# Spectral bank without turns in its slots, and V loads of 96 and 4 rows in neighbourhood attention

## The chip, the cores and the metric

The kernel runs on one core of a Trainium2 chip. The metric is the device time of one execution in microseconds. TensorE is called PE, VectorE DVE, ScalarE ACT, GpSimd POOL and SyncE SP, as in the profile.

## The reference

The input x is (2, 128, 64, 64) in fp32. Four layers in a row each add something to it: neighbourhood attention over 7 x 7 windows (twice, then a layer norm), a convolution attention, linear attention and a spectral filter bank, causal attention and experts. Two of them are changed. Neighbourhood attention, per image, layer and head:

```python
attn = jnp.einsum('bijhd,bijpqhd->bijhpq', q, kw)      # kw, vw: the 7 x 7 windows
attn = softmax(attn + bias over the 49 keys)
out = jnp.einsum('bijhpq,bijpqhd->bijhd', attn, vw) @ w_p.T + b_p
```

The spectral bank takes u (2, 4096, 128), the layer norm of the tokens, and 16 filters phi of 4096 positions:

```python
U_plus = irfft(Vf[None, :, :, None] * Uf_p[:, :, None, :], n=8192)[:, :sl]   # and U_minus with signs
out = einsum('btkd,k,kde->bte', U_plus, s, Mpp) + einsum('btkd,k,kde->bte', U_minus, s, Mpm)
out = out + sum over i < 3 of (u shifted by i) @ Mu[i]                        # three taps
```

This is done for prefixes of four lengths, weighed by a gumbel softmax and summed.

## The kernel before

X, the 128 channels by 2 x 4096 positions, stays on chip for the whole kernel. The stages follow each other with barriers between them. Order is written out by hand: each stage has one program for each engine, and semaphores link them.

**Neighbourhood attention** (`neighbourhood_attention`) has four passes (two layers, two images) of 32 groups each, 128 in all. ACT stores V to DRAM tile by tile (`v_out`, two buffers). SP copies it there into overlapping windows (`group`: 12 DMAs for a quarter of a pass, lines 270 to 273), and loads the windows of each group (`load`, line 282, `na_v`, four buffers, 100 rows of 1040 values). PE multiplies in `values` (line 365). The loads, the window copies and their waits all stand in SP's one queue. Ahead of it all, the input is group normed. PE's part of that is one matmul (line 415), behind the bias tables (lines 401 and 405) in PE's program.

**The spectral bank** replaces the long FFT by blocks: the 4096 positions are 64 blocks of 64 (`NB`, `R`). A transform over the block index gives 64 slots, each slot a pair of rows. In every slot the convolution within blocks is a product with filter rows laid out as a Toeplitz matrix.

- `spectral_inputs` stores u to DRAM (line 1379) and loads it with blocks as rows (line 1384). PE transforms the filters (line 1413) and u (line 1421), DVE drains, SP stores `u_hat`.
- `autoregressive` adds the three taps (line 1723), one loop body per image.
- `spectral_slots` runs the 64 slots, each of 4 chunks (`kc`). PE turns the slot's input (`turn_inputs`, line 1528), multiplies it with the filters (`convolve`, line 1542, into five PSUM banks) and mixes over filters and channels with the mixing weights (`mix`, lines 86 to 88). Values are split in a high and a low fp32r part, and each product is three matmuls. ACT makes the high part of a convolution's result (line 1589), DVE the low part (line 1624), POOL splits the filters. PE convolves a chunk of the next slot while it mixes this slot's, four chunks ahead, and turns the output (`turn_outputs`, line 1562) before SP stores it.
- `spectral_inverse` loads `y_hat` (line 1666), transforms back over blocks and stores it. `spectral_output` loads that with positions as rows, turns it on PE and adds it to X times `keep`, a factor for each 512 positions.

## Time and profile before

| | us |
|---|---|
| median of 3 runs (3557.59 to 3560.82) | 3558.94 |
| the profiled execution | 3560.56 |
| its span in the profile | 3558.8 |
| PE busy | 3162.1 (89%) |
| DVE busy | 1884.2 (53%) |
| ACT busy | 1281.8 (36%) |
| POOL busy | 989.8 (28%) |

Busy is the time in which an engine had an instruction at work. The shares are means over stages that differ: in the profile's slices PE has a 9 (90% or more) all through the slots, and lower digits around them.

### The profile page before, as it was taken

Reading aid. Unit: us, or ns where it says so; the run is one execution under the profiler, and the core shown is the slowest. Engines: PE = TensorE matmul, PEld = TensorE weight load, DVE = VectorE, ACT = ScalarE, POOL = GpSimd, SP = SyncE. Lnnn points to the kernel's source line nnn. Section 1 sums busy time; section 2 is a strip of 40 time slices with the busy share of each in tenths; the row PEclk is TensorE's granted clock in tenths of the full one; section 3 lists DMA queues with packets and bytes.
Section 4 is the critical chain, followed back from the end, with each engine's and each line's share of the span. In section 5 each row is a group of like instructions: output and inputs, shape, how many; then the busy total and the mean of one; then the engine's idle time right before and its main releaser. Section 6 shows DMA issues by size and latency. Waiting matters only on the chain. (4 is left out here: it accounts for less than half of the span.)

```text
span 3558.8 us, 60876 instructions
## 1 busy us (share of the span) xinstructions
PE 3162.1 (89%) x23681; PEld 2437.8 (69%) x23681; DVE 1884.2 (53%) x3818; ACT 1281.8 (36%) x2479; POOL 989.8 (28%) x976
## 2 busy tenths in 40 slices
PE   5998988688864789999999999999788998999799
PEld 4676776233433258888888888888457886888655
DVE  5555565577525345555555555555235554555365
ACT  2554544111222034444444444444233333333300
POOL 3444441277421034444444444444000000000000
PEclk9999999799986899999999999999889999999899
DMA  6877751000012643444434444443410000000000
GB/s 164 178 156 168 157 149 48 12 1 1 1 34 82 219 68 62 73 71 64 75 63 72 71 64 75 65 70 62 154 46 1 1 1 1 1 1 1 8 18 30
DMA packets 431206, 230.12 MB, mean 65 GB/s; under 512 B 328468, under 2 KB 409004, under 8 KB 427724
## 3 DMA queue, kind: packets, MB, share of 16 engines
q1 hardware_dynamic: 408352, 212.60, 29.2%
q10 hardware_dynamic: 22572, 13.63, 1.8%
q8 instruction: 192, 3.15, 0.4%
q14 instruction: 90, 0.74, 0.1%
HBM read 186.20 MB, written 61.28 MB: 70 GB/s over the span
## 5 line engine op out<-in xcount | busy, mean ns | idle before, releaser
L1624 DVE TENSOR_TENSOR sl_vl_slot<-sl_psV_slot,sl_vh_slot 128x512 fp32r<-128x512 f32 x1024 | 635.7, 683 | 553.7 <-ACT sl_vh_slot L1589 553.7
L1589 ACT ACTIVATE sl_vh_slot<-sl_psV_slot 128x512 fp32r<-128x512 f32 x1024 | 529.5, 604 | 536.5 <-PE sl_psV_slot L1542 536.2
L86 PE MATMUL sl_psY_slot<-sl_vl_slot,sp_Mh_sp 128*128 128x256 f32 x2048 | 603.3, 295 | 0.0
L87 PE MATMUL sl_psY_slot<-sl_vh_slot,sp_Ml_sp 128*128 128x256 f32 x2048 | 578.4, 282 | 0.0
L88 PE MATMUL sl_psY_slot<-sl_vh_slot,sp_Mh_sp 128*128 128x256 f32 x2048 | 577.4, 282 | 0.0
L86 PEld LDWEIGHTS sl_psY_slot<-sl_vl_slot,sp_Mh_sp 128*128 128x128 f32 x2048 | 390.0, 190 | 56.3 <-issue 56.3
L1516 POOL CAST sl_fh_slot<-sl_f_slot 128x512 fp32r<-128x512 f32 x256 | 168.7, 659 | 864.2 <-PE sl_psV_slot L1542 686.8
L87 PEld LDWEIGHTS sl_psY_slot<-sl_vh_slot,sp_Ml_sp 128*128 128x128 f32 x2048 | 390.9, 191 | 0.0
L88 PEld LDWEIGHTS sl_psY_slot<-sl_vh_slot,sp_Mh_sp 128*128 128x128 f32 x2048 | 390.3, 191 | 0.0
L1518 POOL TENSOR_TENSOR sl_fl_slot<-sl_f_slot,sl_fh_slot 128x512 fp32r<-128x512 f32 x256 | 338.1, 1321 | 20.5
L1914 PE MATMUL ca_ps_ca<-ca_v_ca,ca_pt_ca 128*128 128x128 f32 x2112 | 285.6, 281 | 25.1 <-ACT ca_pt_ca L2003 14.2
L1914 PEld LDWEIGHTS ca_ps_ca<-ca_v_ca,ca_pt_ca 128*128 128x128 f32 x2112 | 258.2, 194 | 42.2 <-ACT ca_pt_ca L2003 25.8
L1542 PE MATMUL sl_psV_slot<-sl_fl_slot,sl_uh_slot 64*128 64x512 f32 x1024 | 230.6, 447 | 2.1 <-POOL sl_fl_slot L1518 1.1
L2003 ACT ACTIVATE ca_pt_ca<-ca_ps_ca 128x512 f32<-128x512 f32 (+2 forms) x144 | 82.6, 573 | 370.0 <-PE ca_ps_ca L1904 370.0
L1542 PE MATMUL sl_psV_slot<-sl_fh_slot,sl_ul_slot 64*128 64x512 f32 x1024 | 203.7, 394 | 0.0
L1542 PE MATMUL sl_psV_slot<-sl_fh_slot,sl_uh_slot 64*128 64x512 f32 x1024 | 200.4, 388 | 0.0
L691 POOL TENSOR_TENSOR na_s_na<-na_s_na,na_nmax_na 128x400 f32<-128x400 f32 x128 | 109.1, 853 | 278.0 <-DVE na_nmax_na L575 257.7
L1981 DVE COPY ca_pt_ca<-ca_ps_ca 128x512 f32<-128x512 f32 (+1 forms) x144 | 91.0, 632 | 179.5 <-PE ca_ps_ca L1904 178.9
L365 PE MATMUL na_psO_na<-na_v_na,na_pt_na 100*64 100x129 f32 x2048 | 144.9, 285 | 34.7 <-issue 34.7
L1904 PE MATMUL ca_ps_ca<-ident,ca_s_ca 128*128 128x128 f32 x1056 | 156.3, 276 | 4.3 <-ACT ca_s_ca L1993 4.3
L365 PEld LDWEIGHTS na_psO_na<-na_v_na,na_pt_na 100*64 100x64 f32 x2048 | 113.5, 140 | 61.0 <-issue 54.3
L1952 DVE TENSOR_SCALAR_CACHE_REDUCE ca_s_ca<-ca_ps_ca 128x512 f32<-128x512 f32 x224 | 149.0, 688 | 0.8 <-PE ca_ps_ca L88 0.8
(383 smaller groups left out, 5608.1 us busy)
## 6 DMA issues: line engine op xcount, KB each, us to landing
sl_f_slot<-filt_hat SPq DMA_DIRECT2D x256, 256.0 KB, 5.5
na_v_na<-na_windows SPq DMA_DIRECT2D x128, 406.2 KB
na_windows<-na_values SPq DMA_DIRECT2D x160, 113.8 KB, 7.2
na_values<-na_vo_na ACTq DMA_DIRECT2D x32, 260.0 KB, 8.9
u_hat<-fw_o_fwd SPq DMA_DIRECT2D x8, 1024.0 KB, 3.8
sl_u_slot<-u_hat SPq DMA_DIRECT2D x128, 64.0 KB, 2.1
y_hat<-sl_o_slot SPq DMA_DIRECT2D x64, 128.0 KB, 1.8
iv_y_inv<-y_hat SPq DMA_DIRECT2D x8, 1024.0 KB, 12.0
```

Of the source, the lines that this page charges most:

```text
L86: e.matmul(out, lh, rl, start=start, stop=False)
L87: e.matmul(out, ll, rh, start=False, stop=False)
L88: return e.matmul(out, lh, rh, start=False, stop=stop)
L365: mm = e.matmul(psO[side:side + 64, u // 2, u % 2 * 129:(u % 2 + 1) * 129], pt_sb[g % 2][0:NK, u, side:side + 64], v_in[g % NV][0:NK, s, 0 ...
L1516: e.tensor_copy(high, raw).then_inc(S["f_high"], 1)
L1518: e.tensor_tensor(low, raw, high, ALU.subtract).then_inc(S["f_split"], 1)
L1542: mm = e.matmul(psV[(first + par) % NPV][:, :], u_in[u % 2][pu][rows, b, :], f_in[kc][pf][rows, :], start=(x == 0), stop=(x == 2))
L1589: e.activation(v_out(0, kc, q), bank(n), ACT.Copy).then_inc(S["v_high"], 1)
L1624: e.tensor_tensor(v_out(1, kc, q), bank(n), v_out(0, kc, q), ALU.subtract).then_inc(S["v_split"], 1)
L1904: tr = e.transpose(psT[n % 2][:, j * 128:(j + 1) * 128], s_sb[i % 2][:, at:at + 128], T["ident"][:, :])
L1914: mm = e.matmul(psO[i % 2][:, 0:128], pt_sb[n % 3][:, j, :], v_all[:, k, :], start=(k == 0), stop=(k == i))
L1952: e.tensor_scalar(dst, psS[n % 3][:, 0:k], 1.0, None, ALU.mult, ALU.max, accum_out=m)\
```

## The change

In neighbourhood attention each burst of 12 window copies is cut in three parts, and SP issues a V load between them. A V load becomes two DMAs, of 96 rows and of 4. There are five `na_v` buffers for four, four `v_out` buffers for two, and the group norm's matmul stands ahead of the tables.

In the spectral bank `spectral_inputs` no longer goes through DRAM for the blocks. PE turns them: columns of u at a stride of 64 values (256 bytes) are the weights, the identity moves, and the result, after a copy by ACT, is the transform's moving operand. The filters' transform and the taps follow in the same stage. `u_hat` is stored with positions as rows, so a slot needs no turn of its input; POOL splits it. PE runs two chunks ahead instead of four, with six PSUM banks and three buffers each for filters and results. The output is stored as it is, in runs of 256 bytes, and image 0's part is loaded again every eight slots (`load_early`). The last two stages become `spectral_outputs`: y at a stride of 256 bytes is the weights, the inverse matrix times `keep` moves with 64 columns, and DVE adds the result straight into X.

```diff
@@ -185,7 +184,7 @@
     PASSES = [(layer, b) for layer in range(2) for b in range(B)]
     G = PER * len(PASSES)
     STEPS = 3 * NCH
-    NQ, NS, NP, NV = 3, 3, 2, 4
+    NQ, NS, NP, NV, NO = 3, 3, 2, 5, 4
...
-                def group(n, part):
-                    for i in range(2):
-                        e.wait_ge(S["v_stored"][i], 16 * ((n * NCH + 2 * part) // 2 + 1))
+                def group(n, part, third):
+                    if third == 0:
+                        for i in (n * NCH + 2 * part, n * NCH + 2 * part + 1):
+                            e.wait_ge(S["v_stored"][i % NO], 16 * (i // NO + 1))
...
-                    for k in range(WIN):
+                    for k in range(4 * third, min(4 * third + 4, WIN)):
...
+                    if third == 2:
+                        e.dma_start(windows[:, :, 0, :], V[:, 0:WIN, :]).then_inc(S["v_grouped"][part], 16)
+                        e.dma_start(windows[:, :, SUB - 1, :], V[:, W - WIN:W, :]).then_inc(S["v_grouped"][part], 16)
...
+                    keys = T["v_windows"][n, k0:k0 + WIN, :, half * 2 * UNITS:(half + 1) * 2 * UNITS, :].rearrange("r k s d -> (r k) s d")
+                    for rows in (slice(0, 96), slice(96, NK)):
+                        e.dma_start(v_in[g % NV][rows, :, :], keys[rows]).then_inc(S["v_loaded"][g % NV], 16)
...
-                    if g in (NV + 1, NV + 5):
-                        group(0, 2 + g // (NV + 5))
+                    if NV <= g < NV + 6:
+                        group(0, 2 + (g - NV) // 3, (g - NV) % 3)
                     for n in range(1, len(PASSES)):
                         for part in range(PARTS):
-                            if step_slot(n * STEPS + 6 * part + 5) + 4 == g:
-                                group(n, part)
+                            third = g - step_slot(n * STEPS + 6 * part + 5) - 4
+                            if 0 <= third < 3:
+                                group(n, part, third)
+
...
-                    e.wait_ge(S["v_loaded"][g % NV], 16 * (g // NV + 1))
+                    e.wait_ge(S["v_loaded"][g % NV], 32 * (g // NV + 1))
...
+                e.wait_ge(S["mom_done"], 1)
+                e.matmul(psO[:, 1, 0:2 * B], T["gmat"][:, :], mom[:, :, :].rearrange("p b m -> p (b m)"),
+                         start=True, stop=True).then_inc(S["grp_in_psum"], 1)
                 e.wait_ge(S["mask_loaded"], 16 * 9)
                 e.wait_ge(S["pick_done"], 1)
                 tables(0)
-                e.wait_ge(S["mom_done"], 1)
-                e.matmul(psO[:, 1, 0:2 * B], T["gmat"][:, :], mom[:, :, :].rearrange("p b m -> p (b m)"),
-                         start=True, stop=True).then_inc(S["grp_in_psum"], 1)
...
+                def turn(c):
+                    if c >= 2:
+                        e.wait_ge(S["t_copied"], c - 1)
+                    for i in range(SC):
+                        s = c * SC + i
+                        for b in range(B):
+                            blocks = G["U"][:, b, UPAD + s:UPAD + s + (NB - 1) * R + 1:R]
+                            mm = e.matmul(psT[c % 2][b * NB:(b + 1) * NB, (SC - 1 - i) * 128:(SC - i) * 128], blocks,
+                                          T["ident"][:, :], start=True, stop=True)
+                    mm.then_inc(S["t_in_psum"], 1)
+
+                def ring_free(n):
+                    if n >= 4:
+                        e.wait_ge(S["f_dve"] if n % 2 else S["f_act"], (n - 4) // 2 + 1)
+
+                def transform(c):
+                    e.wait_ge(S["t_copied"], c + 1)
+                    for b in range(B):
+                        ring_free(2 * c + b)
+                    for b in range(B):
+                        rows = slice(b * NB, (b + 1) * NB)
+                        e.matmul(ps[(2 * c + b) % 4][:, :], fwd[rows, b, :], turned[c % 2][rows, :], start=True, stop=True)\
+                            .then_inc(S["f_in_psum"], 1)
+
+                e.wait_ge(S["fwd_loaded"], 16)
+                for c in range(NS):
+                    turn(c)
+                    if c >= 1:
+                        transform(c - 1)
+                transform(NS - 1)
                 e.wait_ge(S["phi_loaded"], 32)
+                for n in range(NU, NU + NFT):
+                    part, k0 = divmod(n - NU, 4)
+                    ring_free(n)
+                    e.matmul(ps[n % 4][:, :], flt[:, part, :], phi[:, 4 * k0:4 * k0 + 4, :].rearrange("a k m -> a (k m)"),
+                             start=True, stop=True).then_inc(S["f_in_psum"], 1)
+                for n in range(B * NCH):
+                    b, c = divmod(n, NCH)
+                    if n >= 2:
+                        e.wait_ge(S["ar_added"], n - 1)
+                    for i in range(3):
+                        at = UPAD + c * CH - i
+                        mm = e.matmul(psA[n % 2][:, :], G["Mu"][:, i, :], G["U"][:, b, at:at + CH], start=(i == 0), stop=(i == 2))
+                    mm.then_inc(S["ar_in_psum"], 1)
...
-    NPV = 5
+    CHUNKS = SLOTS * KC
+    NPV, NFI, NVR, EARLY = 6, 3, 3, 8
...
-                    for b in range(B):
-                        e.dma_start(u_raw[u % 2][:, b, :].rearrange("d (i s) -> d i s", i=2), uh[u, :, b, :, :].rearrange("i d s -> d i s"))\
+                    uh = T["u_hat"][2 * u:2 * u + 2, :, :].rearrange("i (s q) c -> q i s c", q=2)
+                    for par in range(2):
+                        e.dma_start(u_raw[u % 2][par * R:(par + 1) * R, :, :].rearrange("p b d -> p (b d)"), uh[par])\
...
+                    for b in range(B):
+                        e.dma_start(T["y_hat"][2 * u:2 * u + 2, b, :, :].rearrange("o e r -> e o r"),
+                                    y_sb[u % 2][:, b * 128:(b + 1) * 128].rearrange("e (o r) -> e o r", o=2))\
+                            .then_inc(S["y_stored"][u % 2], 16)
+
+                def load_early(group):
+                    for i in range(2):
+                        e.wait_ge(S["y_stored"][i], 32 * (EARLY // 2) * (group + 1))
+                    rows = slice(2 * EARLY * group, 2 * EARLY * (group + 1))
+                    e.dma_start(G["y0"][rows, :], T["y_hat"][rows, 0, :, :].rearrange("c e r -> c (e r)")).then_inc(S["y_early"], 16)
...
+                split_input(0)
+                for n in range(CHUNKS):
+                    split_filters(n)
+                    if n % KC == 2 and n // KC + 1 < SLOTS:
+                        split_input(n // KC + 1)
...
-                turn_inputs(0)
-                for kc in range(KC):
-                    convolve(0, kc)
-                turn_inputs(1)
-                for u in range(SLOTS):
-                    for kc in range(KC):
-                        mix(u, kc)
-                        if u + 1 < SLOTS:
-                            convolve(u + 1, kc)
-                        if kc == 1 and u >= 1:
-                            turn_outputs(u - 1)
-                        if kc == 2 and u + 2 < SLOTS:
-                            turn_inputs(u + 2)
-                turn_outputs(SLOTS - 1)
+                convolve(0)
+                convolve(1)
+                for n in range(CHUNKS):
+                    mix(n)
+                    if n + 2 < CHUNKS:
+                        convolve(n + 2)
...
+def spectral_outputs(nc, T, G):
...
+            @block.tensor
+            def _(e):
+                e.wait_ge(S["inv_kept"], 1)
+                for b in range(B):
+                    e.wait_ge(S["yh_loaded"][b], 16 * (NP if b else 1))
+                    for g in range(GROUPS):
+                        n = b * GROUPS + g
+                        if n >= 4:
+                            e.wait_ge(S["i_added"], n - 3)
+                        for i in range(RB):
+                            r = g * RB + i
+                            mm = e.matmul(ps[n % 4][:, i * NB:(i + 1) * NB], y_in[b][:, r:r + (C - 1) * R + 1:R], kept[:, :],
+                                          start=True, stop=True)
+                        mm.then_inc(S["i_in_psum"], 1)
...
+                    x = X[:, b * L:(b + 1) * L].rearrange("e (j r) -> e r j", r=R)[:, g * RB:(g + 1) * RB, :]
+                    e.tensor_tensor(x, ps[n % 4][:, :].rearrange("e (r j) -> e r j", r=RB), x, ALU.add).then_inc(S["i_added"], 1)
...
             spectral_inputs(nc, T, G)
-            autoregressive(nc, T, G)
+        G["y0"] = sb("sp_y0", [128, C * R])
         spectral_slots(nc, T, G)
-        spectral_inverse(nc, T)
-        spectral_output(nc, T, G)
+        spectral_outputs(nc, T, G)
 
```

The order of the instructions moves in these places. First SP's queue in a later pass of neighbourhood attention, where `na_windows` is the DRAM array of overlapping windows, line 270 (before) a copy of one window column and line 282 the load of a group's V. Before:

```order
L282 DMA na_v_na<-na_windows 100x1040 x6
L270 DMA na_windows<-na_values 16x14x130 x10
L272 DMA na_windows<-na_values 160x1x130
L273 DMA na_windows<-na_values 160x1x130
L282 DMA na_v_na<-na_windows 100x1040 x6
```

After:

```order
L285 DMA na_v_na<-na_windows 96x1040
L285 DMA na_v_na<-na_windows 4x1040
L270 DMA na_windows<-na_values 16x14x130 x4
L285 DMA na_v_na<-na_windows 96x1040
L285 DMA na_v_na<-na_windows 4x1040
L270 DMA na_windows<-na_values 16x14x130 x4
L285 DMA na_v_na<-na_windows 96x1040
L285 DMA na_v_na<-na_windows 4x1040
L270 DMA na_windows<-na_values 16x14x130 x2
L273 DMA na_windows<-na_values 160x1x130
L274 DMA na_windows<-na_values 160x1x130
```

Where twelve copies stood in one run, four at most do, with a load in two pieces between.

Then PE in a slot, at the two chunks with extra work. `sl_psV` is the result of a convolution, `sl_psY` the mix, `sl_psU` the turned input. Before:

```order
L1542 MATMUL sl_psV_slot<-sl_fh_slot,sl_uh_slot 128x512 x2
L1562 MATMUL sl_psY_slot<-ident,sl_y_slot 128x128 x2
L86 MATMUL sl_psY_slot<-sl_vl_slot,sp_Mh_sp 128x256
...
L1542 MATMUL sl_psV_slot<-sl_fh_slot,sl_uh_slot 128x512 x2
L1528 MATMUL sl_psU_slot<-ident,sl_u_slot 64x128 x4
L86 MATMUL sl_psY_slot<-sl_vl_slot,sp_Mh_sp 128x256
```

After, in every chunk:

```order
L87 MATMUL sl_psY_slot<-sl_vh_slot,sp_Mh_sp 128x256
L1617 MATMUL sl_psV_slot<-sl_fl_slot,sl_uh_slot 128x512 x2
L1617 MATMUL sl_psV_slot<-sl_fh_slot,sl_ul_slot 128x512 x2
...
L1617 MATMUL sl_psV_slot<-sl_fh_slot,sl_uh_slot 128x512 x2
L85 MATMUL sl_psY_slot<-sl_vl_slot,sp_Mh_sp 128x256
```

Between a convolution and the next mix nothing is left; lines 85 to 87 are lines 86 to 88 of before.

Last PE in the input stage, from its first matmul to the taps. Before, with the taps (line 1723) in a loop body of a stage of their own:

```order
L1413 MATMUL fw_ps_fwd<-fw_phi_fwd,fw_flt_fwd 128x512 x8
L1421 MATMUL fw_ps_fwd<-fw_u_fwd,fw_m_fwd 128x512 x32
L69 UNCONDITIONAL_BRANCH
L1715 UNCONDITIONAL_BRANCH
L1717 UNCONDITIONAL_BRANCH
L1723 ISA
L1723 MATMUL ar_ps_ar<-sp_U_sp,sp_Mu_sp 128x512
```

After, where `fw_psT` is a turned tile, `fw_t` its copy and `ar_ps` the taps:

```order
L1429 MATMUL fw_psT_fwd<-ident,sp_U_sp 64x128 x16
L1443 MATMUL fw_ps_fwd<-fw_t_fwd,fw_m_fwd 128x512 x2
L1429 MATMUL fw_psT_fwd<-ident,sp_U_sp 64x128 x8
...
L1443 MATMUL fw_ps_fwd<-fw_t_fwd,fw_m_fwd 128x512 x4
L1456 MATMUL fw_ps_fwd<-fw_phi_fwd,fw_flt_fwd 128x512 x8
L1464 MATMUL ar_ps_fwd<-sp_U_sp,sp_Mu_sp 128x512 x48
```

The turns alternate with transforms, and the filters have moved from the front to behind them.

## Rows read from the trace of the kernel before

**Rows 1.** Windows: busy us (instructions) of PE, PEld, DVE, ACT, POOL; clock, DMA share, GB/s
```profile
60.00:596.00 536.00, 482.98 (x6261) 370.91 (x6260) 301.74 (x680) 271.22 (x671) 233.81 (x253) 0.96 0.70 152
...
1152.00:1222.80 70.80, 39.91 (x80) 17.01 (x80) 27.20 (x41) 0.00 (x0) 0.00 (x0) 0.74 0.85 285
...
1600.00:1900.00 300.00, 300.00 (x2391) 256.02 (x2391) 163.89 (x278) 138.63 (x279) 122.78 (x124) 1.00 0.44 69
2525.50:2576.00 50.50, 32.29 (x64) 9.66 (x64) 10.84 (x16) 9.33 (x16) 0.00 (x0) 0.82 0.77 250
```

**Rows 2.** Timeline at the start: start us, us, engine, line, operation [idle before]
```profile
23.21 0.16 DVE L636 COPY gn_mom_na<-gn_mv_na 128x2 f32<-128x2 f32 x1
...
30.45 0.59 PE L415 MATMUL na_psO_na<-gn_mom_na,gmat 128*128 128x4 f32 x2
...
32.38 0.42 POOL L682 TENSOR_SCALAR na_b_na<-na_b_na 128x1 f32<-128x1 f32 x2 [31.93 <-DMA na_w_na<-in_na_w]
...
41.81 0.69 DVE L549 TENSOR_TENSOR na_vo_na<-na_psT_na,na_bv_na 128x512 f32<-128x512 f32 x1
...
63.89 0.69 DVE L549 TENSOR_TENSOR na_vo_na<-na_psP_na,na_bv_na 128x512 f32<-128x512 f32 x1 [6.16 <-DMA na_values<-na_vo_na]
```

**Rows 3.** Groups by line, 60 to 596 us: busy us, mean ns | idle before
```profile
L365 PE MATMUL na_psO_na<-na_v_na,na_pt_na 100*64 100x129 f32 x2048 | 144.9, 285 | 34.7 <-issue 34.7
```

**Rows 4.** Timeline of SP's DMA queue around one burst
```profile
144.97 7.41 SPq L270 DMA_DIRECT2D na_windows<-na_values  x10
...
153.82 13.61 SPq L282 DMA_DIRECT2D na_v_na<-na_windows  x6
```

**Rows 5.** Windows, a stretch of V loads between two bursts
```profile
220.00:247.00 27.00, 27.00 (x357) 20.40 (x353) 15.47 (x37) 15.96 (x39) 13.59 (x16) 1.00 0.47 132
```

**Rows 6.** Timeline of the input transform and the taps
```profile
1152.85 12.72 SPq L1379 DMA_DIRECT2D u_blocks<-sp_U_sp  x2
...
1186.43 30.49 PE L1421 MATMUL fw_ps_fwd<-fw_u_fwd,fw_m_fwd 128*128 128x512 f32 x64 [16.91 <-DMA fw_u_fwd<-u_blocks]
...
1247.61 20.87 PE L1723 MATMUL ar_ps_ar<-sp_U_sp,sp_Mu_sp 128*128 x48 [2.26 <-PEq L71]
...
1270.23 0.89 SPq L1482 DMA_DIRECT2D sl_u_slot<-u_hat  x2
```

**Rows 7.** Timeline of PE in a slot, at the starts of chunks
```profile
1856.36 0.50 PE L1542 MATMUL sl_psV_slot<-sl_fl_slot,sl_uh_slot 64*128 64x512 f32 x2
...
1861.00 0.50 PE L1542 MATMUL sl_psV_slot<-sl_fl_slot,sl_uh_slot 64*128 64x512 f32 x2
...
1862.58 0.44 PE L1562 MATMUL sl_psY_slot<-ident,sl_y_slot 128*128 128x128 f32 x2
...
1865.81 0.50 PE L1542 MATMUL sl_psV_slot<-sl_fl_slot,sl_uh_slot 64*128 64x512 f32 x2
...
1867.39 0.66 PE L1528 MATMUL sl_psU_slot<-ident,sl_u_slot 128*64 128x128 f32 x8
...
1871.04 0.50 PE L1542 MATMUL sl_psV_slot<-sl_fl_slot,sl_uh_slot 64*128 64x512 f32 x2
```

**Rows 8.** Timeline of DVE, the splits of one chunk
```profile
1858.04 2.48 DVE L1624 TENSOR_TENSOR sl_vl_slot<-sl_psV_slot,sl_vh_slot 128x512 fp32r<-128x512 f32 x4 [2.16 <-ACT sl_vh_slot L1589]
```

**Rows 9.** Timeline of the inverse, its first load and matmul, and the next stage's first instruction
```profile
2525.86 4.12 SPq L1666 DMA_DIRECT2D iv_y_inv<-y_hat  x8
...
2531.07 13.39 PE L1704 MATMUL iv_ps_inv<-iv_y_inv,iv_m_inv 128*64 128x512 f32 x24 [8.35 <-DMA iv_m_inv<-in_c_inv]
...
2602.30 0.30 DVE L780 MEMSET ln_rows_ca<- 64x128 f32 x2 [1.10 <-PEq L71]
```

**Rows 10.** The router's matmuls in the timeline, and the windows' row of a part
```profile
3364.16 13.79 PE L2066 MATMUL ex_psL_ex<-ex_rw_ex,Y 128*128 128x8 f32 x64 [11.34 <-PEq L71]
...
3370.00:3373.00 3.00, 3.00 (x16) 3.00 (x15) 0.00 (x0) 0.00 (x0) 0.00 (x0) 0.50 0.02 5
...
3405.21 1.85 PE L2066 MATMUL ex_psL_ex<-ex_rw_ex,Y 128*128 128x8 f32 x16
```

More of the change, by code:

```diff
@@ L45 @@
 SLOTS = NB
-SPB = 8
 MOE = 8
@@ L620, in _ @@
                               row_head[:, :].unsqueeze(2).to_broadcast([128, HEADS, HD])).then_inc(S["fold_done"], 1)
-                for i in range(2):
+                for i in range(NO):
                     op = e.memset(v_out[i][:, :, 128:VW], 1.0)
@@ L1406, in _ @@
             def _(e):
-                e.wait_ge(S["phi_loaded"], 32)
-                for n in range(8 + NP * 4):
-                    if n >= 4:
-                        e.wait_ge(S["f_copied"], n - 3)
-                    if n < 8:
-                        part, k0 = n // 4, (n % 4) * 4
-                        e.matmul(ps[n % 4][:, :], flt[:, part, :], phi[:, k0:k0 + 4, :].rearrange("a k m -> a (k m)"),
-                                 start=True, stop=True).then_inc(S["f_in_psum"], 1)
-                    else:
-                        b, c = divmod(n - 8, NP * 2)
-                        if n == 8:
-                            e.wait_ge(S["fwd_loaded"], 16)
-                        if b == 0 and c % 4 == 0:
-                            e.wait_ge(S["u_loaded"][c // 4], 16)
-                        e.matmul(ps[n % 4][:, :], fwd[:, b, :], u_blk[:, c * CH:(c + 1) * CH], start=True, stop=True)\
-                            .then_inc(S["f_in_psum"], 1)
+                def turn(c):
[8 more added lines that the diff above has]
+                    mm.then_inc(S["t_in_psum"], 1)
@@ new lines, in _, with copy_turned, copy_spectrum @@
+                for n in range(B * NCH):
[6 more added lines that the diff above has]
+                    mm.then_inc(S["ar_in_psum"], 1)
+            @block.scalar
+            def _(e):
+                def copy_turned(c):
+                    e.wait_ge(S["t_in_psum"], c + 1)
+                    if c >= 2:
+                        e.wait_ge(S["f_in_psum"], 2 * (c - 1))
+                    e.activation(turned[c % 2][:, :], psT[c % 2][:, :], ACT.Copy).then_inc(S["t_copied"], 1)
+                def copy_spectrum(n):
+                    e.wait_ge(S["f_in_psum"], n + 1)
+                    piece_free(e, n)
+                    dst, src = spectrum(n)
+                    e.activation(dst, src, ACT.Copy).then_inc(S["f_act"], 1)
+                for c in range(NS):
+                    copy_turned(c)
+                    if c >= 1:
+                        copy_spectrum(2 * (c - 1))
+                for n in range(NU - 2, NU + NFT, 2):
+                    copy_spectrum(n)
@@ L1441, in spectral_slots @@
+                for n in range(B * NCH):
+                    c = n % NCH
+                    e.wait_ge(S["ar_in_psum"], n + 1)
+                    x = X[:, n * CH:(n + 1) * CH]
+                    e.scalar_tensor_tensor(x, psA[n % 2][:, :], G["keep"][:, c:c + 1], x, ALU.mult, ALU.add).then_inc(S["ar_added"], 1)
 def spectral_slots(nc, T, G):
     KC, KN = 4, NF // 4
-    PER = 4 * KC
-    NPV = 5
+    CHUNKS = SLOTS * KC
+    NPV, NFI, NVR, EARLY = 6, 3, 3, 8
     HALF = R // 2
@@ L1597, in outputs @@
+                        e.activation(v_out(0, n, q), bank(4 * n + q), ACT.Copy).then_inc(S["v_high"], 1)
                 def outputs(u):
@@ L1608, in _ @@
-                inputs(1)
-                for u in range(SLOTS):
-                    for kc in range(KC):
-                        if kc == KC - 1:
-                            outputs(u)
-                        if u + 1 < SLOTS:
-                            high(u + 1, kc)
-                        if kc == 2 and u + 2 < SLOTS:
-                            inputs(u + 2)
+                                 psY[u % 2][:, :].rearrange("p (q n r) -> p q n r", q=2, r=HALF), ACT.Copy).then_inc(S["y_out"], 1)
@@ L1618, in _ @@
+                for n in range(CHUNKS):
+                    high(n)
+                    if n % KC == 0 and n >= KC:
+                        outputs(n // KC - 1)
+                outputs(SLOTS - 1)
             @block.vector
             def _(e):
-                def low(u, kc):
+                for n in range(CHUNKS):
                     for q in range(4):
-                        n = PER * u + 4 * kc + q
-                        e.wait_ge(S["v_high"], n + 1)
-                        e.tensor_tensor(v_out(1, kc, q), bank(n), v_out(0, kc, q), ALU.subtract).then_inc(S["v_split"], 1)
```

355 lines of the change are left out of this document (116 added, 239 removed).

## The prediction

> **What bounds the kernel now.** I read the windows by stage first [rows 1]; the number after a stretch's length is TensorE's (PE's) busy time. PE works 483 of the 536 us of neighbourhood attention, all 300 of a 300 us stretch of the slots, but 40 of 71 us in the input transform and 32 of 50 in the inverse. So there are different limits. In the slots every PE instruction that goes is time that goes, if nothing else becomes late. In the transform and the inverse PE waits for round trips through DRAM (DMA share 0.85 and 0.77), and what counts is when data lands. In the attention PE is the bound except in its stalls. Then I read the timelines around each edit for durations, and the groups by line for the stalls.
>
> The sum is made against the profiled execution: a span of 3558.8 us, 3560.56 us in all, 1.6 above the median of 3558.94.
>
> **Attention, start: -7 us (bounds -2 and -7).** The group norm's matmul runs at 30.45, behind the tables, though its input was ready at 23.4 [rows 2]. Moved ahead of them, it and the norm behind it can start 7 us earlier. But the projections need the weights as well, which land at about 32.3 (when POOL first uses them [rows 2]), so less than 7 is left: the first V tile, drained at 41.81 [rows 2], would come near 37.1, -4.7. Then the seventh V tile's drain waited 6.16 us for a store of one of two buffers [rows 2]. Four buffers remove that; I let 2.3 us of it reach PE's first groups. If the weights hide the first part, -2 remains.
>
> **Attention, stalls: -34 us (bounds 0 and -50).** PE idles 34.7 us in front of the V matmuls [rows 3], in 14 stalls of 0.6 to 6.0 us, each behind a burst: SP issues 12 window DMAs from 144.97 on and reaches the V loads only at 153.82 [rows 4], 8.9 us later, where a group takes 536/128 = 4.2 us. The order shows what changes: a burst is cut in thirds of 4 with a V load between them, a load is two pieces, and a fifth V buffer gives 4.2 us more lead. In a stretch with V loads only, the DMA share is 0.47 and PE works without a gap [rows 5]: the loads leave half of the engines free, so thirds of a burst should fit between. Besides the idle time, the clock is 0.96 over the stage [rows 1], 21 us missing, of which I put 8 on the stalls (estimate). (34.7 + 8) x 0.8 = 34. Zero if DMA is the bound after all; 50 with all of both and more of the clock.
>
> The Trainium skill (DMA: Bandwidth & Descriptors, Why a DMA increments its semaphore by 16 and not by 1) says that a transfer goes over the largest number of engines, up to 16, that divides its rows: 10 for 100 rows, 16 for 96. By this a load's data would land up to a third sooner, and the whole 42.7 us would be the sum's term in place of 34. The trace's share of 0.47 for loads alone agrees with ten engines of 16.
>
> **Inputs and taps: -22 us (bounds -31 and -12).** From the first store at 1152.85 to the slots' first load at 1270.23 are 117.4 us [rows 6]: 33.6 until the transform begins (blocks to DRAM and back, the filters' transform under it), 30.5 of transform, the rest taps in two loop bodies. After, a round of four positions (16 rounds) is:
> - the turn, 16 PE instructions. In the slots, the chunk with eight of this kind (64 columns as weights, 128 moving) lasts 5.23 us, one without 4.64 [rows 7]: 0.59 for eight, 1.18 for 16.
> - the transform, two matmuls of 512 columns with 64 rows each. A tap matmul costs 20.87/24 = 0.87 (x48 counts two instructions for each) [rows 6]. In the slots the two 64-row halves of the array overlap: 12 instructions of 512 columns between 1861.00 and 1862.58 [rows 7] are 0.13 each. 0.87 for two if they overlap here, 1.74 if not; I take the middle, 1.29.
>
> A round is 2.47, all 39.5. The stores aren't the bound: they moved 8 MB in the 30.5 us before. ACT's and DVE's drains, two to three of some 0.7 us a round over two engines, lie under PE. Then 8 filter matmuls, 8 x 0.87 = 6.9, and the taps, 48 x 0.87 = 41.7; start 3, cold clock 2.6 (estimate: 5 us at clock 0.50, which the router's start shows [rows 10]), end 2. Sum 95.7. Overlap or none moves it by 7 either way (89, 103), turns at 0.8 or 1.1 of their price by 4 and 2, to 85 and 105.
>
> **Slots: -47 us (bounds -40 and -50).** Starts of chunks stand at 1856.36, 1861.00, 1865.81 and 1871.04 [rows 7]: 4.64 without extras, 4.81 with the output's two transposes, 5.23 with the four input turns. A slot is 2 x 4.64 + 4.81 + 5.23 = 19.32, without extras 18.56. Both extras go, as the order shows: 64 x 0.76 = 48.6, less 1.6 since POOL now splits the first input before PE can start. The price of a shorter lead: DVE's four splits of a chunk run from 1858.04 to 1860.52 [rows 8], and its convolution ended at some 1857.9, so they are done 2.6 us after it. Two chunks ahead, PE comes back to them one period, 4.64, after the convolution's end: 2.0 us of slack. Six banks for five keep the convolution's own wait as far. POOL works 122.8 of 300 us [rows 1], 7.9 of a slot in four splits of 1.97; u, half as wide, adds 1.0 to a slot of 18.56. These hide it; without them each us would count.
>
> **Inverse and output: -39 us (bounds -10 and -45).** From 2525.86 to 2602.30 are 76.4 us [rows 9] of load, transform, store, load and turn. After: 5 us until the last 512 KB of image 0 are there (the first matmul of before came 5.2 after its load's issue [rows 9]), then 128 matmuls, 256 instructions, with 128 columns as weights and 64 moving. The nearest rows are the router's, 128 columns as weights and 8 moving: 16 instructions in 1.85 at full clock, 0.116 each, and 64 in 13.79 at clock 0.50, 0.215 each [rows 10]. At 0.11 they take 28, with 2 for a cold start and 2.5 for the last add 37.8. Image 1's 4 MB land in 15 us by the rate of the transform's stores (8 MB in 30.5), under the 5 and image 0's 14. DVE's 16 adds of some 0.7, strided maybe 1.4, stay under a group's 1.8. At 0.215 it is 55 and the gain 12.
>
> **Sum.** -7 - 34 - 22 - 47 - 39 = -149. 3560.6 - 149 = 3411.6, by the median 3410.
>
> **Rivals.**
> - **Weights at a stride, or a cold clock, double the inverse.** No matmul of before reads 128 weight columns 256 bytes apart; the turns and the inverse do. And the router's first 64 instructions stayed at clock 0.50 for 14 us with PE busy throughout [rows 10]. At 0.215 the inverse costs 25 more (3435); turns doubled too, 16 x 1.18 = 19 more (3454). Against: before them PE has worked through 1200 us of slots, and 64 columns move where the router moves 8. Chance 0.22.
> - **The DMA engines bound the attention.** If the copies and not SP's order make V late, cutting the burst changes nothing: 3410 + 34 = 3444. For: the mean share is 0.70 over the stage [rows 1]. Against: 0.47 between bursts [rows 5]. Chance 0.15.
> - **Slower: the two-chunk lead is too short.** If the splits come late, PE waits in each of 256 chunks; from 149/256 = 0.58 us a chunk on the kernel is slower, which takes splits 2.6 us later than in rows 7 and 8. At 0.65 us it would be 3410 + 166 = 3576. Chance 0.03.
> - **The extras don't leave the slots.** The order excludes it.
>
> The Trainium skill (Advanced Engine Details and Errata, Memory Cachelines) has a rule that speaks for the first rival: SBUF is read in lines of 16 bytes, and a pattern whose every access falls in another line pays a penalty. Each weight column 256 bytes on would be such an access. The page names no price for weights and no row here has one; doubled, the time would be that rival's 3435 to 3454.
>
> **How the numbers follow.** The forecast (its own range 3385 to 3430) 0.58, first rival 0.22, second 0.15, slower 0.03, a loss elsewhere 0.02. Below 3382 the gains would all have to be at their far ends, above 3458 two rivals at once. A difference under 0.2%, 7 us, can't be told from none here. All but the slower case are faster, with a little off for mishaps together: 0.96, same 0.01, slower 0.03.
>
> **What would show it.** In the profile after: under 10 us of idle time before the V matmuls, the first V drain near 37; some 95 us between the norm's end and the slots' first load, in rounds of 2.5; chunks of 4.64 throughout, slots of 18.56; an inverse of 38 us at 0.11 per instruction. It is wrong if the transform's halves don't overlap, the inverse runs at half clock, PE has gaps in the slots, or the attention's stalls only move.

## The result, and the profile after

The changed kernel takes 3429.45 us (median of four runs, 3425.23 to 3431.88) against 3559.24 us for the kernel before on the same chip: a ratio of 0.9632, 95% interval [0.9617, 0.9647], 129.8 us less. The forecast was 3410 with a range of 3382 to 3458. The profiled execution took 3425.23 us with a span of 3423.2, so its sum below is some 4 us better than the median.

The first and last instruction of each part, read from both timelines, show where the time went:

| from | to | before | after | change | forecast |
|---|---|---|---|---|---|
| start | first DMA of the input stage | 1152.85 | 1105.60 | -47.3 | -41 |
| there | the slots' first load | 117.4 | 89.3 | -28.0 | -22 |
| there | the inverse's first load | 1255.6 | 1206.5 | -49.2 | -47 |
| there | first instruction of the next norm | 76.4 | 65.4 | -11.1 | -39 |
| there | end of the span | 956.5 | 956.4 | -0.1 | 0 |

Three parts came out at their forecast or 6 us better. The inverse gave 11 us of its 39.

The start of the attention in DVE's timeline of the changed kernel (start, duration, engine, line, operation), and the group of V matmuls by line, 60 to 590 us (busy, mean ns, idle time before); they answer to [rows 2, 3]:

```profile
23.32 0.16 DVE L643 COPY gn_grp_na<-na_psO_na 128x4 f32<-128x4 f32 x1 [0.74 <-PE na_psO_na L417]
...
36.16 0.69 DVE L554 TENSOR_TENSOR na_vo_na<-na_psT_na,na_bv_na 128x512 f32<-128x512 f32 x1
```

```profile
L370 PE MATMUL na_psO_na<-na_v_na,na_pt_na 100*64 100x129 f32 x2048 | 140.9, 279 | 3.9 <-issue 3.3 <-ACT na_pt_na L486 0.7
```

The first V tile is drained 5.7 us earlier, the eighth 7.2 us (57.5 for 64.7), and no drain waits for a store. Of the 34.7 us before the V matmuls 3.9 are left. The attention's last matmul ends at 528.2 where it ended at 575.4, so 47.1 us of the first row's 47.3 were won in the attention.

The input stage in PE's timeline, answering to [rows 6]. A turn of 16 instructions and a transform of 4 alternate:

```profile
1116.06 1.18 PE L1429 MATMUL fw_psT_fwd<-ident,sp_U_sp 128*64 128x128 f32 x16
1117.17 1.13 PE L1443 MATMUL fw_ps_fwd<-fw_t_fwd,fw_m_fwd 64*128 64x512 f32 x4
1118.23 1.19 PE L1429 MATMUL fw_psT_fwd<-ident,sp_U_sp 128*64 128x128 f32 x16
```

A round takes 1118.23 - 1116.06 = 2.17 us: 1.11 for the turn, which is 0.07 per instruction, and 1.06 for the transform. All 16 rounds take 36.8 us (1108.25 to 1145.07), since the granted clock was 0.50 up to 1114; that is 2.1 more than 16 x 2.17.

Starts of the chunks in a slot, PE's timeline, answering to [rows 7]:

```profile
1861.30 0.50 PE L1617 MATMUL sl_psV_slot<-sl_fl_slot,sl_uh_slot 64*128 64x512 f32 x2
...
1865.94 0.50 PE L1617 MATMUL sl_psV_slot<-sl_fl_slot,sl_uh_slot 64*128 64x512 f32 x2
...
1870.58 0.50 PE L1617 MATMUL sl_psV_slot<-sl_fl_slot,sl_uh_slot 64*128 64x512 f32 x2
```

Each period is 4.64, with no longer one among them. DVE's splits start at 1858.35 and 1862.98 and still take 2.48. So they are done 2.0 us before PE comes back to them, as the prediction worked out from [rows 8]. It called this slack, and it is called the cover below.

The inverse in PE's timeline, answering to [rows 9], and its windows (length, busy us and instructions of PE, PEld, DVE, ACT, POOL, granted clock, DMA share, GB/s), with a stretch of the input stage and one of the slots ahead:

```profile
2408.76 28.09 PE L1706 MATMUL iv_ps_inv<-iv_k_inv,sp_y_sp 128*128 128x64 f32 x128 [10.92 <-DVE iv_k_inv L1713]
2436.65 28.04 PE L1706 MATMUL iv_ps_inv<-iv_k_inv,iv_y_inv 128*128 128x64 f32 x128
```

```profile
1118.00:1149.00 31.00, 31.00 (x255) 17.63 (x254) 10.57 (x16) 16.74 (x28) 0.00 (x0) 1.00 0.64 263
...
1600.00:1900.00 300.00, 300.00 (x2329) 256.67 (x2328) 159.98 (x258) 139.55 (x275) 144.22 (x161) 1.00 0.50 75
...
2400.00:2409.00 9.00, 0.24 (x1) 0.24 (x2) 0.23 (x1) 0.00 (x0) 0.00 (x0) 0.55 0.76 141
...
2413.00:2437.00 24.00, 24.00 (x112) 24.00 (x111) 8.36 (x8) 0.00 (x0) 0.00 (x0) 0.50 0.18 76
2437.00:2465.00 28.00, 27.69 (x128) 27.50 (x127) 10.11 (x9) 0.00 (x0) 0.00 (x0) 0.50 0.00 1
```

256 instructions take 56 us, 0.219 each, at a granted clock of 0.50 from end to end, with PE busy all the time. That is the price of the first rival, and the two causes which it named together had to be taken apart: the clock and the stride.

### The profile page after: what moved, and what is told of

Same layout as the page of the kernel before. It is cut to its first block and busy times, and to the rows that moved or that the text cites. A ratio compares the mean times of both kernels' runs of the same rounds, so it can differ in the third digit from the quotient of the medians.

```text
span 3423.2 us, 60243 instructions
## 1 busy us (share of the span) xinstructions
PE 3109.1 (91%) x23425; PEld 2431.8 (71%) x23425; DVE 1828.6 (53%) x3657; ACT 1276.4 (37%) x2435; POOL 1056.2 (31%) x1104
## 5 line engine op out<-in xcount | busy, mean ns | idle before, releaser
L1617 PEld LDWEIGHTS sl_psV_slot<-sl_fl_slot,sl_uh_slot 64*128 64x128 f32 x1024 | 96.2, 184 | 61.5 <-issue 15.4
```

The lines of the kernel that those rows point to most:

```text
L1617: mm = e.matmul(psV[(first + par) % NPV][:, :], u_in[u % 2][pu][rows, b, :], f_in[n % NFI][pf][rows, :], start=(x == 0), stop=(x == 2))
```

## The experiments

The twelve runs were made on three chips beside the kernel before, which took 3579.1, 3584.3 and 3569.4 us there. Times are therefore compared within a chip or as ratios to before, and stages by their own length in the traces. The length of the inverse is counted from its first load to the first instruction of the next norm: 65.4 in the changed kernel. The price of an instruction there is the duration of a row of 128 (one image) divided by 128, unless another row is named: 28.04/128 = 0.219 in the changed kernel. The window counts are not used for it, because they include the instructions that overlap a window's edges.

**Neighbouring columns as weights.**

```diff
...
-    y_in[b][:, r:r + (C - 1) * R + 1:R], kept[:, :],
+    y_in[b][:, r * 128 % (C * R):r * 128 % (C * R) + 128], kept[:, :],
...
```

> The changed kernel with one edit: the inverse's weights are 128 neighbouring columns of y instead of 128 columns 256 bytes apart (so the output of the spectral bank is not the reference's; the work is the same in count and shape). Clock theory (the inverse costs 0.218 us per instruction because the clock is 0.50, the stride is free): the inverse stays at 56 us and the whole at 3429, plus or minus 5. Stride theory (each strided column costs a second read, the clock is only a by-product): 256 instructions at 0.11 = 28 us, the whole 3401.

Measured: a ratio of 0.9644 [0.9624, 0.9663], and an inverse of 64.4 us.

```profile
2434.84 27.57 PE L1706 MATMUL iv_ps_inv<-iv_k_inv,sp_y_sp 128*128 128x64 f32 x128 [10.97 <-DVE iv_k_inv L1713]
2462.20 27.52 PE L1706 MATMUL iv_ps_inv<-iv_k_inv,iv_y_inv 128*128 128x64 f32 x128
```

An instruction takes 27.52/128 = 0.215 us at clock 0.50. The stride theory alone falls: without any stride the inverse costs the same but for 1 us. The clock is enough to explain it, but it needn't be the only limit.

**128 moving columns.**

```diff
...
+    cols = 2 * NB if i < RB - 1 else NB
-    mm = e.matmul(ps[n % 4][:, i * NB:(i + 1) * NB], y_in[b][:, r:r + (C - 1) * R + 1:R], kept[:, :],
+    mm = e.matmul(ps[n % 4][:, i * NB:i * NB + cols], y_in[b][:, r:r + (C - 1) * R + 1:R], kept[:, 0:cols],
...
```

> The changed kernel with the matrix kept doubled side by side: each matmul of the inverse moves 128 columns instead of 64, the second 64 of which the next matmul overwrites (the last of eight moves 64). Same result, twice the moving columns per weight load. Clock theory in its first form (few moving columns per weight load are what keeps the clock at 0.50): the clock rises to 1.00 some microseconds into the stage, an instruction costs about 0.12, the inverse about 32 and the whole 3405. In its second form (only the idle 9 us ahead of the stage count): the clock stays 0.50, instructions cost 0.22 or a little more, the whole 3429 to 3435. Stride theory: not below 3429.

Measured: a ratio of 0.9633 [0.9602, 0.9664], an inverse of 66.6 us. The two images in PE's timeline, and windows of this kernel, with the columns as above:

```profile
2438.25 28.32 PE L1707 MATMUL iv_ps_inv<-iv_k_inv,sp_y_sp 128*128 128x128 f32 x128 [11.61 <-DVE iv_k_inv L1715]
2466.41 28.27 PE L1707 MATMUL iv_ps_inv<-iv_k_inv,iv_y_inv 128*128 128x128 f32 x128
```

```profile
2440.00:2442.00 2.00, 2.00 (x11) 2.00 (x11) 0.00 (x0) 0.00 (x0) 0.00 (x0) 0.50 1.01 418
2442.00:2446.00 4.00, 4.00 (x20) 4.00 (x20) 1.72 (x2) 0.00 (x0) 0.00 (x0) 0.89 0.99 410
2446.00:2470.00 24.00, 24.00 (x111) 24.00 (x111) 8.26 (x7) 0.00 (x0) 0.00 (x0) 1.00 0.04 16
```

The first matmul starts at 2438.25, and between 2442 and 2446 the clock rises to 1.00; with 64 moving columns it had stood at 0.50 for the whole stage. And the time doesn't move: an instruction of the second image takes 28.27/128 = 0.221 us, at twice the clock. The clock did what the first form of the clock theory said, the time what the stride theory said; no expectation had both together. A second limit of nearly the same size lies behind the clock.

**PE at work ahead of the inverse.** Eight matmuls of 512 columns (identity times X, into a bank of its own) run while the stage waits for its first load. 3.6 us of idle time are left between the slots and them.

```diff
+                for i in range(8):
+                    e.matmul(psW[:, :], T["ident"][:, :], X[:, 0:CH], start=True, stop=True)
                 e.wait_ge(S["inv_kept"], 1)
```

> The changed kernel with 8 extra matmuls of 512 columns (identity times X, into an unused bank) on PE while the inverse waits for its first load, about 7 us at full clock, so that PE isn't idle between the slots and the inverse. Second form of the clock theory (the idle time ahead lets the clock fall, and it stays where it is): the inverse runs at 1.00, about 29 us, whole 3402. First form (few moving columns don't hold the clock): the inverse begins at 1.00 and falls to 0.50 after a few us; the inverse 50 to 56 us, whole 3422 to 3431.

Measured: a ratio of 0.9662 [0.9643, 0.9680], an inverse of 67.7 us. PE's timeline and the windows:

```profile
2444.64 27.89 PE L1709 MATMUL iv_ps_inv<-iv_k_inv,sp_y_sp 128*128 128x64 f32 x128
2472.33 28.03 PE L1709 MATMUL iv_ps_inv<-iv_k_inv,iv_y_inv 128*128 128x64 f32 x128
```

```profile
2446.00:2448.00 2.00, 2.00 (x11) 2.00 (x11) 0.00 (x0) 0.00 (x0) 0.00 (x0) 1.00 1.02 418
2448.00:2450.00 2.00, 2.00 (x11) 2.00 (x10) 1.24 (x1) 0.00 (x0) 0.00 (x0) 1.00 1.00 418
2450.00:2472.00 22.00, 22.00 (x103) 22.00 (x102) 7.47 (x6) 0.00 (x0) 0.00 (x0) 0.52 0.05 20
```

The inverse began at 2444.6 at full clock and kept it for some 6 us; then it fell to 0.50 with PE busy throughout. So the idle time ahead is not what keeps the clock down in this stage. And full clock bought nothing: from 2445.1 to 2450.4, all at 1.00, 25 instructions start, 0.218 us apart, and in the second image, all at 0.50, one takes 28.03/128 = 0.219. Weights at a stride cost 0.22 at either clock. The stage is even 2.3 us longer than in the changed kernel, as the extra matmuls, themselves partly at clock 0.50, took 10 us and not 7.

**Both edits of the weights and the columns.** The first two edits together.

> Both edits of the inverse at once: weights from 128 neighbouring columns (so the spectral bank's output is not the reference's) and 128 moving columns. What stands so far: neighbouring columns alone left 0.214 us per instruction at clock 0.50, 128 moving columns alone brought the clock to 1.00 and left 0.22. Two-limits theory (half clock and strided weights each cost about as much, and either hides the other): 0.12 to 0.13 per instruction once the clock is up, the inverse 34 us for 56, whole 0.6% below the changed kernel. Rival (a third limit, for instance DVE's strided adds into X or the bank they share): 0.2 per instruction again, no gain.

Measured: a ratio of 0.9574 [0.9550, 0.9598], an inverse of 41.0 us. PE's timeline of the two images:

```profile
2437.85 17.00 PE L1707 MATMUL iv_ps_inv<-iv_k_inv,sp_y_sp 128*128 128x128 f32 x128 [11.16 <-DVE iv_k_inv L1715]
2454.68 14.46 PE L1707 MATMUL iv_ps_inv<-iv_k_inv,iv_y_inv 128*128 128x128 f32 x128
```

The second image, all at full clock, takes 14.46/128 = 0.113 us per instruction, where the strided one took 0.221 at the same clock and the same columns. This shows two limits of one size, each hiding the other: the half clock (0.215 with neighbouring columns) and the strided read of 128 weight columns (0.218 to 0.221 at full clock). Taking either away alone gives at most 1 us. The rival, a third limit in DVE's adds, falls.

**A version with the result of the reference.** ACT, idle in this stage, copies eight positions of y at a time so that a position's channels are neighbours.

```diff
...
+    e.activation(tile[n % 3][:, :, :], y_in[b][:, :].rearrange("c (e r) -> c r e", r=R)[:, g * RB:(g + 1) * RB, :], ACT.Copy)
...
-    y_in[b][:, r:r + (C - 1) * R + 1:R], kept[:, :],
+    tile[n % 3][:, i, :], kept[:, 0:cols],
...
```

> A version with the reference's output: ACT, idle in the inverse, copies each group of eight positions of y into a tile where a position's 128 channels are neighbours (16 copies of 128x1024, read at the stride), PE takes its weights from there, and 128 columns move. Two-limits theory: ACT's copy of 1024 elements is some 1.2 us, under PE's 2.0 per group, so the inverse takes 35 to 38 us with the first copy in front, whole 18 to 22 us below the changed kernel (0.5 to 0.6%). Rival (the strided read costs ACT as it costs PE): 2.3 us or more per copy, the inverse 40 us or more, gain 15 or less.

Measured: a ratio of 0.9568 [0.9545, 0.9591] and 3428.7 us on a chip where before took 3584.3; an inverse of 43.1 us, 22.3 less than the changed kernel's. ACT's row (eight copies of an image):

```profile
2435.10 15.19 ACT L1720 ACTIVATE iv_t_inv<-sp_y_sp 128x1024 f32<-128x1024 f32 x8 [10.19 <-DMA sp_y_sp<-y_hat]
2450.20 16.77 ACT L1720 ACTIVATE iv_t_inv<-iv_y_inv 128x1024 f32<-128x1024 f32 x8
```

A copy costs 1.9 to 2.1 us on average, not the 1.2 assumed. That speaks for a price of the strided read on ACT too, but no run has the same copy without the stride. It is near the 1.8 (14.46/8) that PE needs for a group, so of the inverse's 24.4 us with both limits away 22.3 are kept. The expectation mixed two cases here: the gain is the one it gave to the two-limits theory, the inverse of 43.1 us lies where it put the rival, and not at 35 to 38.

**Further additions to it.** The inverse matrix loaded first, five extra matmuls ahead, six V buffers in the attention.

```diff
-    NQ, NS, NP, NV, NO = 3, 3, 2, 5, 4
+    NQ, NS, NP, NV, NO = 3, 3, 2, 6, 4
...
+                for i in range(5):
+                    e.matmul(psW[:, :], T["ident"][:, :], X[:, 0:CH], start=True, stop=True)
```

> The version with ACT's copies and 128 moving columns in the inverse (which took 31.7 us for 256 instructions), and three additions: the small inverse matrix is loaded ahead of y and not behind it, five extra matmuls of 512 columns keep PE busy while it waits, and the attention has six V buffers for five. By the two-limits theory the copies bring 22 us against the changed kernel, the full clock from the start 2, the earlier matrix up to 2. A sixth buffer gives one more group of lead, 4.2 us per burst: if the stalls come from lateness in bursts, half of the 20 to 25 us on such a chip goes (total -35 against the changed kernel); if the DMA engines are short over whole stretches, the buffer gives nothing (total -24).

Measured: a ratio of 0.9612 [0.9596, 0.9628] against 0.9631 [0.9614, 0.9647] for the changed kernel on the same chip, some 7 us and not the 24 or more expected; the intervals overlap. The traces place the loss in the inverse and in the attention:

```profile
2432.98 17.23 ACT L1723 ACTIVATE iv_t_inv<-sp_y_sp 128x1024 f32<-128x1024 f32 x8 [11.02 <-DMA sp_y_sp<-y_hat]
2450.11 17.89 ACT L1723 ACTIVATE iv_t_inv<-iv_y_inv 128x1024 f32<-128x1024 f32 x8
```

The inverse took 47.1 us, 4 more than without the additions. PE is at full clock from the start, but ACT sets the pace, with 2.2 us per copy, and PE waits 0.2 to 0.3 us for it in most groups. Why a copy takes 2.2 here and 1.9 to 2.1 before is open. The matrix loaded first brings nothing either: ACT's first copy starts 7.5 us after y's load is issued, 7.1 without the additions. And with six buffers the input stage begins 11.8 us later than in the changed kernel on that chip, 8.5 of them there by the attention's last matmul, with 18.7 us of idle time for 11.7. A sixth buffer doesn't help.

**The changed kernel once more,** as the measure for its chip.

> The changed kernel itself, unchanged, as the measure for the other three on one chip. 3429 to 3455, a ratio of 0.963 to 0.964 to the kernel before; if the idle time before the V matmuls is 20 us and more here as in the last eight runs and not the 3.9 of the first trace, the difference is between chips and not between edits, and its size shows in the time.

Measured: a ratio of 0.9631 [0.9614, 0.9647], the same as on the first chip. But 11.7 us stand idle before the V matmuls here, 3.9 there, and 20 to 26 on the two chips of the eight other runs wherever the attention was left as changed. What remains of the stalls differs from chip to chip. One trace isn't exact here either: in the three inverse experiments of one chip, whose attention is the same program, the input stage begins at 1131.9, 1133.9 and 1139.4.

**The burst whole again.** All 12 window copies are issued where the first third was.

> The changed kernel with the 12 window copies of a burst again in one run (all else kept: V loads of 96 and 4 rows, five V buffers, four store buffers). If the cut into thirds is what removed the stalls before the V matmuls: 20 to 35 us of idle time are back, 3450 to 3465. If the 16-engine loads and the fifth buffer did it: under 8 us of idle time, 3429 to 3437.

Measured: a ratio of 0.9743 [0.9722, 0.9763], against 0.9633 to 0.9662 for the three inverse experiments on the same chip, which left the attention alone. The attention and what follows up to the input stage ended 20 to 27 us later than in these three. The V matmuls, and SP's queue around the burst:

```profile
L372 PE MATMUL na_psO_na<-na_v_na,na_pt_na 100*64 100x129 f32 x2048 | 147.7, 288 | 44.2 <-issue 44.2
```

```profile
145.70 6.40 SPq L270 DMA_DIRECT2D na_windows<-na_values  x10
152.14 0.60 SPq L273 DMA_DIRECT2D na_windows<-na_values  x1
152.79 0.60 SPq L274 DMA_DIRECT2D na_windows<-na_values  x1
153.55 14.29 SPq L285 DMA_DIRECT2D na_v_na<-na_windows  x12
```

44.2 us are idle for 20 to 26. Nearly 8 us without a V load stand in SP's queue again. The loss is well above the 7.5 us by which the three differ among themselves. The cut into thirds is the larger part of the gain; five buffers and 96-row loads don't stand in for it.

**V loads of 100 rows again.** The two DMAs of 96 and 4 rows become one of 100.

```diff
-                    for rows in (slice(0, 96), slice(96, NK)):
+                    for rows in (slice(0, NK),):
```

> The changed kernel with each V load in one DMA of 100 rows again instead of 96 and 4 (thirds, five V buffers and four store buffers kept). If the order in SP's queue is what counts: no change, 0 to 8 us. If the spread over more engines counts: idle time before the V matmuls grows by 10 to 30 us and the kernel by as much. The measured 24 us of idle time left on this chip in the runs before (3.9 on the first) say that DMA is close to a bound, which speaks for the second.

Measured: a ratio of 0.9655 [0.9632, 0.9678]. The two inverse kernels on this chip have the attention as changed, and their inverses are 22 to 24 us shorter; with 23/3584 = 0.0064 added to their 0.9568 and 0.9574, the changed kernel would stand at 0.9632 to 0.9638. The interval begins at 0.9632, so the times alone don't tell the two apart. In the traces the input stage begins 10.0 and 11.7 us later than in these two, and 9.7 later than in the kernel with one chunk ahead (below), the third on this chip with the attention as changed. Idle time before the V matmuls is 26.5 for 21.1, 24.4 and 24.1. The three others lie within 2 us of each other. So the split loads are worth some 10 us by one trace against three, of which only 2 to 5 show as that idle time; that it is the number of engines that counts is not shown.

**Four V buffers.** `NV` is 4 instead of 5.

> The changed kernel with four V buffers instead of five. If the lead of a group is what the fifth buffer gives: 4.2 us less lead for each burst of which there are 16, idle time before the V matmuls up by 10 to 30 us. If the cut bursts alone do it: within 3 us of the changed kernel.

Measured: a ratio of 0.9615 [0.9598, 0.9633], with the changed kernel's 0.9631 on the same chip. The intervals overlap; its trace has 7.3 us of idle time for 11.7. The fifth buffer gives nothing that can be measured.

**The start of the attention as before.** The group norm's matmul stands behind the tables again, and two buffers store V.

> The changed kernel with the start of the attention as before: the group norm's matmul behind the tables again and two buffers for storing V. The sum gave these two 7 us, and the trace after shows the eighth V tile 7.2 us earlier than before. Expected 5 to 8 us slower than the changed kernel (0.15 to 0.23%); if the weights' landing or later stalls hide it, 0 to 2.

Measured: a ratio of 0.9659 [0.9644, 0.9675] against 0.9631 [0.9614, 0.9647], intervals that just touch. In the traces the first V matmul starts at 77.9 for 70.3, and the input stage begins 7.3 us later (1125.34 for 1118.04). The 7.7 us at the first V matmul are the 7 of the sum; before and after the change it stands at 77.2 and 70.1.

**One chunk ahead.** PE convolves chunk n + 1 behind the mix of n and not n + 2.

```diff
-                convolve(1)
...
-                    if n + 2 < CHUNKS:
-                        convolve(n + 2)
+                    if n + 1 < CHUNKS:
+                        convolve(n + 1)
```

> The changed kernel with the convolution only one chunk ahead of the mix instead of two: PE then mixes a chunk right behind its convolution and waits for ACT's and DVE's split of it. The slack of two chunks (splits done 2.6 us after the convolution, needed 4.64 after it) says: each of 256 chunks waits 2.6 us, 665 us more, 4095 to 4120, with a lower clock on top. If the slots had been bound by something else: much less.

Measured: 4354.3 us in its one run. PE's wait in a chunk:

```profile
1861.83 0.39 PE L85 MATMUL sl_psY_slot<-sl_vl_slot,sp_Mh_sp 128*128 128x256 f32 x1 [2.57 <-DVE sl_vl_slot L1669]
```

The wait is 2.57 us, as the slack had said. The whole rose by more than 256 x 2.57 = 658, and by more than the 4095 to 4120 expected: the slots alone take 2104.5 us for 1206, 3.5 more per chunk. The mean clock over 300 us of slots was 0.86, and part of the mixes stand at 0.21 us per instruction in place of 0.12. The chunk from 1857.60 to 1866.29 took 8.7 us where the wait alone would make 7.2.

## Why the prediction was right, and where it was not

**Attention, start** (-7). It held: -7.2 at the eighth V tile, and 7.3 us in the experiment that undid it. That the weights' landing bounds the first part held too: the norm's result was there 7.8 us earlier (23.32 for 31.08 at DVE's first copy), but PE's first projection waited for the weights and began at 31.60 for 34.50, 2.9 earlier, and the first drain came 5.7 earlier.

**Attention, stalls** (-34). 47.3 - 7.2 = 40 came on the first chip, above the term and below its bound of 50. 31 of the 40 are idle time before the V matmuls that is gone; the other 9 lie elsewhere in the attention, and the granted clock over it is 0.97 for 0.96. The reason was right in its first half. Whole bursts alone cost 20 to 27 us, 100-row loads some 10 by one trace. The fifth buffer, to which the text gave 4.2 us of lead, gives nothing. The rival of the DMA engines was put at the wrong place: it doesn't decide whether the cut pays, but how much idle time is left, 4 to 26 us by chip. The reading of the share of 0.47 in [rows 5] as "ten engines of 16" also fails. In the same window (220 to 247 us) a kernel with 100-row loads showed 0.53, and those with 96 and 4 rows on that chip 0.54 and 0.55, so the share of a stretch doesn't tell how many engines a load uses. The 4.2 us for a group were too long as well, as the window of 536 us runs on past the attention's end at 575.4: from the first V matmul (77.2) to the last (571.8) it is 3.9. The rule of the Trainium skill (DMA: Bandwidth & Descriptors, Why a DMA increments its semaphore by 16 and not by 1) that 96 rows go over 16 engines and 100 over 10 fits the 10 us of the split, but no row here shows the engines of one load.

**Inputs and taps** (-22, measured -28). The turn was right (1.11 for 1.18). The transform's halves of 64 rows overlap: two matmuls take 1.06 and not the 1.29 taken between 0.87 and 1.74. With the turn that is 16 x 0.3 = 4.8 us for a round of 2.17 and not 2.47. The cold start cost 2.1 us for 2.6; its 5 us at half clock stood in no row, since the router's first 64 instructions ran so for 14. The term of the transform was mis-sized by taking the middle, where the row of the slots' half-array matmuls said that they overlap.

**Slots** (-47, measured -49). Chunks of 4.64 throughout, and the cover of 2.0 us holds. The run with one chunk ahead shows what the cover is worth.

**Inverse and output** (-39, measured -11). The step that failed is "At 0.11 they take 28": they took 56 at 0.219. The 28 stood on the router's row at full clock with weights that are neighbours, and neither held. The load took 7.4 us and not 5: DVE waited for the small matrix until 2408.48, 7.1 us after the stage's first load, and y lands no sooner (ACT waited 7.1 us for it in the version with copies). The text weighed the router's row at clock 0.50 against 1200 us of full work ahead and 64 columns for 8. The run with PE at work ahead began at full clock and fell to 0.50 after 6 us; the run with 128 columns rose to 1.00 and stayed there. The other half of the rival, the stride, was true as well and for itself enough: with the clock at 1.00 an instruction with strided weights still took 0.218 to 0.221, one with neighbours 0.113. The turns in the input stage, with 64 weight columns at the same stride and 128 moving, showed no such doubling, 0.07 per instruction at clock 1.00, as in the slots of before with columns 8 bytes apart (0.59 for eight). So the price of the stride doesn't carry from one shape to the other. The rule of the Trainium skill (Advanced Engine Details and Errata, Memory Cachelines) pointed the right way for the inverse, and not for the turns. DVE's adds (1.24 us where unstrided ones took 0.68 to 0.75) and ACT's copies (1.9 to 2.2 for 1024 elements where 512 take 0.6) agree with it, but no run took the stride away from them.

The forecast of 3410 was 19 us below the median. Against the profiled execution the sum is this: 3411.6, 28 more for the inverse, 6 less each for the attention and the input stage, 2 less for the slots, 3425.6 for the 3425.2 measured. That the median lies in the forecast's own range of 3385 to 3430 is in part luck: the inverse missed by 28 us, the first rival's price, and 14 us won elsewhere hid half of it.

## What to carry to other kernels

When two limits of one size stand behind a row, removing either shows nothing: test them together before calling either harmless. Look at the granted clock of a stage even where PE is busy without a gap: with 64 moving columns against 128 weight columns it stood at 0.50 here, as in the router's first 64 instructions with 8, and with 128 moving it rose to 1.00. Moving twice the columns cost 1 us of 56 while the weights were strided, and halved the time once they were neighbours in SBUF. And where one queue issues both bulk copies and the loads that something waits for, cut the bulk into pieces between the loads before adding buffers.

## What was not expected of the hardware

- With 128 moving columns and strided weights the inverse took 0.221 us per instruction at clock 1.00; with 64 and strided weights 0.219 at clock 0.50 and 0.218 at clock 1.00; with 64 and neighbouring weights 0.215 at clock 0.50; with 128 and neighbouring weights 0.113 at clock 1.00.
- With 64 moving columns the clock fell to 0.50 while PE was busy without a gap, some 6 us after the stage began at 1.00; with 128 columns it rose from 0.50 to 1.00 between 4 and 8 us after the first matmul.
- The attention as changed left 3.9, 11.7 and 20 to 26 us of idle time before the V matmuls on different chips, while the slots, bound by PE, took 1206 us on each.
